# Key, key, sum, sum: regrouping the steps of a cross-attention loop on four engines, and a rewritten opening

## The reference

```
lat = layer_norm(latents, ln_lat_g, ln_lat_b)
ctx = layer_norm(context, ln_ctx_g, ln_ctx_b)
q = (lat @ Wq)                    # 16 heads of 64
k, v = split(ctx @ Wkv)           # 1024 tokens per batch
k = apply_rope(k, cos, sin)       # rotation of the two halves of each head
attn = clip(q k^T * scale, -11, 11); attn = softmax(attn)
out = (attn v) @ Wo + bo
```

## Time and profile before

| | |
|---|---|
| median of 3 runs | 1251.46 us (1250.63 to 1252.29) |
| the profiled execution | 1255.13 us, of it 1253.4 us span |
| PE busy | 95% of the span |
| DVE / POOL / ACT busy | 78% / 56% / 52% |
| opening, up to the first scores | 67.4 us |
| loop of the steps | to about 960 us |
| linear attention, then experts | to about 1073 us, then to the end |

### The profile page before, as it was taken

One profiled execution on the slowest core, in us unless ns is written; L12 is line 12 of the kernel. 1 busy time (PEld: TensorE's weight loads), 2 busy tenths in 40 slices (PEclk: granted clock), 3 DMA queues, 4 the chain that ended last, 5 costly groups with the idle time before them and its releaser, 6 DMA issues.

```text
span 1253.4 us, 39825 instructions
## 1 busy us (share of the span) xinstructions
PE 1191.6 (95%) x16268; PEld 1003.6 (80%) x16268; DVE 981.2 (78%) x1954; ACT 646.7 (52%) x1089; POOL 700.2 (56%) x611
## 2 busy tenths in 40 slices
PE   7798999999999999999999999999999999899997
PEld 3576878878877888778878878778878888789997
DVE  6489878878878888888888878778868366668886
ACT  7364455655545545555555545555435233356664
POOL 2374767757667766667767756666434123333333
PEclk8899999999999999999999999999999999999999
DMA  6264656656555665556655656655654441566662
GB/s 228 51 160 109 164 134 149 156 138 153 137 132 140 159 155 138 144 139 160 152 132 141 162 136 149 148 133 132 156 126 110 148 157 36 186 182 194 203 189 68
DMA packets 136173, 181.36 MB, mean 145 GB/s; under 512 B 30316, under 2 KB 96312, under 8 KB 135864
## 3 DMA queue, kind: packets, MB, share of 16 engines
q1 hardware_dynamic: 110552, 150.80, 45.5%
q10 hardware_dynamic: 21360, 23.80, 7.5%
q0 software_dynamic: 4080, 4.22, 1.6%
HBM read 81.93 MB, written 30.56 MB: 90 GB/s over the span
## 4 chain that ended last, share of the span: by engine, by line
PE 87%; issue 3%; DVE 3%; ACT 2%; DMA 2%; POOL 1%; SPq 1%; POOLq 0%; ACTq 0%; DVEq 0%
PE bank L1560 29%; PE bank L1589 27%; PE bank L1546 10%; PE bank L1915 6%; PE bank L1612 3%; PE bank L1719 2%; PE bank L1965 2%; PE bank L1966 1%; PE bank L1967 1%; PE bank L1772 1%; PE bank L1647 1%; PE bank L1815 1%; PE bank L1796 1%; DMA w_two<-in_L_ffn_W_dram 1%; DMA x_slots<-xn_all,slot 1%
## 5 line engine op out<-in xcount | busy, mean ns | idle before, releaser
L1560 PE MATMUL bank<-ct,wk_hi 128*128 128x512 f32 x1024 | 332.7, 407 | 11.0 <-DVE ct L1117 4.2
L1589 PE MATMUL bank<-p_hi,xc 128*128 128x512 f32 x1024 | 316.0, 390 | 0.0
L597 POOL TENSOR_TENSOR kr<-kr,ksw 128x1024 f32<-128x1024 f32 x64 | 154.7, 2417 | 186.8 <-issue 140.3
L1107 DVE TENSOR_TENSOR kw<-bank,stab 128x512 f32<-128x512 f32 x256 | 176.4, 689 | 100.7 <-PE bank L1560 95.3
L1560 PEld LDWEIGHTS bank<-ct,wk_hi 128*128 128x128 f32 x1024 | 192.9, 193 | 53.5 <-issue 8.8
L1589 PEld LDWEIGHTS bank<-p_hi,xc 128*128 128x128 f32 x1024 | 191.8, 188 | 39.8
L1560 PE MATMUL bank<-ct,wk_lo 128*128 128x512 f32 x512 | 204.9, 400 | 0.0
L1589 PE MATMUL bank<-p_lo,xc 128*128 128x512 f32 x512 | 199.2, 389 | 0.0
L779 ACT CAST p_hi<-pr 128x1024 fp32r<-128x1024 f32 x128 | 133.7, 1045 | 88.1 <-DVE pr L1075 87.8
L609 POOL TENSOR_TENSOR xc<-raw,xc 128x255 fp32r<-128x255 f32 x128 | 167.0, 1304 | 1.3 <-ACT xc L742 1.3
L1095 DVE TENSOR_TENSOR p_lo<-pr,p_hi 128x1024 fp32r<-128x1024 f32 x128 | 165.6, 1294 | 0.5 <-ACT p_hi L779 0.5
(11 more groups left out here) (227 smaller groups left out, 1994.9 us busy)
## 6 DMA issues: line engine op xcount, KB each, us to landing
ksw<-kw SPq DMA_DIRECT2D x512, 128.0 KB, 2.3
x_turned<-xt SPq DMA_DIRECT2D x120, 128.0 KB, 3.3
ct_read<-x_turned SPq DMA_DIRECT2D x30, 512.0 KB, 5.1
w_two<-in_L_ffn_W_dram SPq DMA_DIRECT2D x15, 1024.0 KB, 5.1
raw<-in_ctx_dram ACTq DMA_DIRECT2D x56, 256.0 KB, 3.6
x_slots<-fill ACTq DMA_DIRECT2D x32, 258.0 KB, 3.8
w_all<-in_L_ffn_W_dram SPq DMA_DIRECT2D x4, 2048.0 KB, 16.9
wo<-in_L_ffn_W_dram SPq DMA_DIRECT2D x7, 1024.0 KB, 5.0
```

The costliest lines, as they stand in the source:

```text
L597: pool.tensor_tensor(kr_at(j + 2), kr_at(j + 2), ksw[:, i], ALU.add).then_inc(kr_done, 1)
L1107: dve.tensor_tensor(by_tile(kw[:, i, cols]), keys_, by_tile(stab[:, places]), ALU.mult).then_inc(kw_done, 1)
L1560: last = pe.matmul(psK[:, a * 512:(a + 1) * 512], l[:, k, w], ct[:, h % 3, r, k], start=(m == 0), stop=(m == len(parts) - 1))
L1589: last = pe.matmul(psZ[c], xc[:, slot_, l, t, cols], r[:, i, :, t], start=(f == 0 and m == 0), stop=(f == 1 and m == len(parts) - 1), skip ...
```

## The change

It moves instructions and changes one wait; no instruction is added or taken away.

- PE, `two_steps`: keys(j+4), keys(j+5), sums(j-2), sums(j-1).
- DVE, `two_steps`: the four `keys_turned` stand in one run; `clamped(j+1)` and `weights_low(j)` come behind them; the odd step's `blocks_turned` moves behind the pair's end, to the head of the next pair; `half_low` comes ahead of `weights_low(j+1)`.
- POOL: the two sums of a pair (`keys_summed`) stand together ahead of the small work (`deviations`) and the low rows (`rows_low`). The first of them waits for `clamp_done` of the pair's first step instead of for `k_ps`, the second for neither.
- the opening: on PE keys(0) stands ahead of the context tile 6, query slices lie between keys(1) and keys(2); ACT, DVE and POOL are written out to match.

```
@@ POOL
-            def step(j):
+            def keys_summed(j):
                 if there(j + 2):
                     pool.wait_ge(ku_done, 2 * (j + 3))
-                    if j >= 0:
-                        if there(j + 4):
-                            pool.wait_ge(k_ps, 2 * (j + 4) + 1)
-                        else:
-                            pool.wait_ge(clamp_done, j + 1)
+                    if j >= 0 and j % 2 == 0:
+                        pool.wait_ge(clamp_done, j + 1)
                     pool.wait_ge(sw_ld[i], ((j + 2) // 2 + 1) * 64)
...
+            for j in range(-5, 0):
+                deviations(j)
+                rows_low(j)
+                keys_summed(j)
+            for j in range(0, STEPS, 2):
+                keys_summed(j)
+                keys_summed(j + 1)
+                for a in range(2):
+                    deviations(j + a)
+                    rows_low(j + a)
@@ ACT, opening
-            opening(-3)
+            rows_high(-4)
+            context_high(6)
+            queries(7, 0)
+            context_high(7)
+            normalised(-4)
+            queries(0, 1)
+            rows_high(-3)
             act.wait_ge(w_last_ld, 32)
             act.activation(w_last[:], w_last[:], ACT.Identity, scale=g_last[:]).then_inc(bias_done, 1)
-            opening(-2)
-            queries(7, 0)
-            queries(0, 1)
-            opening(-1)
             queries(1, 1)
+            normalised(-3)
+            rows_high(-2)
             queries(2, 1)
+            normalised(-2)
+            rows_high(-1)
             queries(3, 1)
+            normalised(-1)
+            loads(-1)
@@ DVE
             def two_steps(j):
+                blocks_turned(j - 1)
                 if due(j, 8):
                     added((j - 8) // 4)
...
                 keys_turned(j, 0)
                 keys_turned(j, 1)
+                keys_turned(j + 1, 0)
+                keys_turned(j + 1, 1)
                 clamped(j + 1)
                 weights_low(j)
                 blocks_turned(j)
...
                 counted(j + 1)
-                keys_turned(j + 1, 0)
-                keys_turned(j + 1, 1)
-                weights_low(j + 1)
-                blocks_turned(j + 1)
                 if half_written(j - 1):
                     half_low(half_written(j - 1))
+                weights_low(j + 1)
@@ DVE, opening
+            keys_turned(-4, 0)
+            keys_turned(-4, 1)
+            context_low(5)
+            shifts(-3)
+            counted(-3)
+            keys_turned(-3, 0)
+            keys_turned(-3, 1)
+            context_low(6)
+            blocks_turned(-3)
+            context_low(7)
+            query_weights_low(1)
...
@@ PE
                 keys(j + 4)
+                keys(j + 5)
                 sums(j - 2)
-                keys(j + 5)
                 sums(j - 1)
...
-            turn_context(6)
             pe.wait_ge(q_act, 6)
             pe.wait_ge(wk_lo_done, 2)
             keys(0)
+            turn_context(6)
             keys(1)
+            queries(7, 0)
             turn_context(7)
-            queries(7, 0)
             queries(0, 1)
+            queries(1, 1)
             keys(2)
-            queries(1, 1)
             queries(2, 1)
             keys(3)
             queries(3, 1)
...
             keys(4)
+            keys(5)
             queries(4, 1)
             queries(5, 1)
-            keys(5)
```

53 lines of the change are left out of this document (23 added, 30 removed).

## The result

The changed kernel takes **1296.95 us** (median; 1293.06 to 1300.1), the kernel before beside it 1251.05. The ratio is 1.037, with an interval of 1.033 to 1.041: 46 us slower, where the forecast was 16 and its range ended at 1290. The sign was right, the size was not. The profiled execution is 1297.26 us, of it 1295.5 span; before it was 1255.13 and 1253.4.

What follows compares the result with a forecast made beforehand. PE's own stream bounds the loop; the opening has real gaps. Terms -9.5 - 4 + 16.5 + 13 = +16 on the median 1251.5 gave 1267.5 us, range 1244 to 1290 (forecast's own 1259 to 1278).

Steps and rivals of the forecast that it cites:

- `o_part`: Loop, keys behind outputs: late x_turned delays `added`, so keys wait 1.0 us in 13 of 29 pairs; +13 us (0 to 28).
- DVE did not become the bound: Loop: a rival had DVE becoming the bound or the clock falling, +24, 1291 us; chance 0.18.
- the first scores end near 60: Opening: both first scores end at 60.0 us instead of 69.5, after waiting for POOL's sum.
- Rival 1: Loop: x_turned lands 4 us from first issue, so `added` is in time; 1254.5 us, chance 0.20.
- Keys on keys: Loop, second keys directly behind first: PE waits for DVE's reading, 0.3 us in about 55 pairs; +16.5 us (8 to 25).
- The worry that the clock would fall more often: Loop, in the rival at 1291 us (chance 0.18): waits before keys plus shorter issue gaps drop PE's clock, 1.8 us each.
- Issue gaps: Loop, inside the scores: gaps stay unchanged because scores and outputs keep their places in PE's stream; 0 us.
- The first pairs: First pairs after the opening: 4 of 6.8 us of PE's waits for DVE and low clock gained; -4 us (0 to -7).
- The opening: Up to the first scores' end: the new order fills PE's gaps; -9.5 us (-12 if POOL's sum is not late, -5 with low clock).

Runs made afterwards that it cites:

- e12: Kernel before with one added wait: SP issues the four x_turned DMAs only when the pair's second keys have run on PE; 1249.85 us (1.0021).
- e5: Changed kernel with DVE's even transpose at the pair's head, x_turned DMAs ahead of the even ksw, ct_read between the two ksw; 1263.22 us (1.0106).
- e10: e5 with two matmuls of sums(j-2) set between keys(j+4) and keys(j+5) on PE; 1244.5 us (0.9974).
- e4: Kernel before with the new opening alone on all engines, and the old loop; 1238.34 us (0.9921).
- e1: Changed kernel with DVE's even-step transpose moved from behind the rotations to the head of the pair; 1274.18 us (1.0227).
- e8: Kernel before with GpSimd's part of the change alone: two sums in one run, the first behind the clamp; 1299.12 us (1.0391).

## Why the prediction was wrong

**Right.** PE's loop was the bound and lost what it gained ahead of it; the wait behind outputs ends with DVE's `o_part` at S+2.8 or later, by the chain of transposes, x_turned and `added`; DVE did not become the bound; the first scores end near 60 (61.3), with POOL's sum as the last wait. Rival 1, the DMA in time, is out for this kernel: it landed 5.3 us from its first issue (median of 28), against 5.0 in the forecast and 5.1 before. What the Trainium skill says in "Perfetto Trace Analysis", section "DMA Instruction — HWDGE (DVE, Sync)", that the completion of writes to HBM can come surprisingly late, agrees with that. But e12 shows that it isn't a constant. In the old loop, issued 3.6 us ahead of the scores (changed kernel 2.8, before 5.3; medians), the same writes were there in 4.4 us, and `o_part` in time. SP and DVE of e12:

```profile
606.84 2.30 SPq L436 DMA_DIRECT2D x_turned<-xt  x4
```

```profile
611.21 0.45 DVE L1072 STREAM_TRANSPOSE xt<-raw 128x256 f32<-128x256 f32 x1 [1.70 <-DMA x_turned<-xt]
```

**Wrong, term by term** (forecast, measured):

- *`o_part`: +13, +23.0.* Two factors. The step that took the wait as 1.0 us in each pair was short: it is 1.45 where it is paid, since the landing is 0.3 us later than 5.0 and the issue 0.2 later than I had it (medians). And the 13 of 29 pairs rested on 16 gap pairs hiding the wait. One of the 16 was miscounted, since its gap (1.76 us at 526.89) lies inside the keys and hides nothing ahead of them; of the other 15 only 11 are left, so 18 pairs have no cover, and 16 of them pay. Three pairs more at 1.0 us are 3 of the 10 us that were missing; the longer wait is the other 7.
- *Keys on keys: +16.5, about +20.5* (e5 to e10). The mechanism was right: 0.18 of waiting and a fresh start. But it is 0.35 a pair and not 0.3, and it was paid in about all 58 pairs and not in 55. The remaining 14.0 us behind the keys (34.5 - 20.5) are nearly those of before (15.0): in both kernels 5 pairs are below the full clock, and e4, where none is, still has 6.8. The worry that the clock would fall more often did not come true.
- *Issue gaps: 0, +5.1.* The step "the gaps stay, since scores and outputs stand at the same places of PE's stream" failed in both halves. The places stayed, but four gaps vanished and the others grew by half. What is fixed in the stream is where a new block of PE's instructions begins; the gap's length, and whether there is one, go with the end of the 16 KB packet on the `instruction` queue, and its start moved from 0.90 us ahead of the gap to 0.13 behind it (seven gaps). The profile of before already had the queue and its packets, and the forecast read "issue" as waiting for nothing that the profile names. The DMA load beside the scores grew as well (share 1.09 and 0.91 in the second and third microsecond behind their start, mean of the 29 pairs; before 0.53 and 0.37); that this delayed the packets is not shown. In e1 the x_turned writes go out 6.1 us ahead of the scores, but `ct_read` (512 KB) then goes out beside their start, and the gaps stay at 31.0.
- *The first pairs: -4, +1.6.* PE's waits in the opening and the first pairs, from its timeline (compare):

```profile
37.72 0.73 PE L1578 MATMUL bank<-ct,wk_hi 128*128 128x512 f32 x2 [0.35 <-DVE kr_third L1118]
45.65 0.70 PE L1578 MATMUL bank<-ct,wk_hi 128*128 128x512 f32 x2 [0.25 <-DVE ct L1123]
59.77 1.54 PE L1564 MATMUL bank<-qo,kr 64*64 64x64 f32 x64 [4.62 <-POOL kr L594]
81.28 0.74 PE L1578 MATMUL bank<-ct,wk_hi 128*128 128x512 f32 x2 [2.05 <-DVE kr L1118]
97.23 0.73 PE L1578 MATMUL bank<-ct,wk_hi 128*128 128x512 f32 x2 [2.48 <-DVE kr_third L1118]
```

  The long waits for `ct` of the earlier trace rows are gone, but in the first pairs two for the readings (2.05 and 2.48) took their place: with both keys in a row, a late DVE meets PE within one half instead of within three. I had priced what goes and not what this lateness meets next. The waits for DVE are still less than before in sum (4.5 us, before 0.51, 1.24 and 3.69). What makes it +1.6 is keys on keys (some 0.35 in each of the four pairs up to scores(8)) and the low clock, met twice (granted clock 0.90 in 61.3:73.8 and in 89.7:107.2) where it was met once (0.91 in 108.9:128.3).
- *The opening: -9.5, -8.2.* As forecast, 1.3 us short, by the one wait of 4.62 for POOL.
- Not in the sum: +1.0 behind the loop, and 4 us because the profiled execution of before lay above its median and that of after does not.

The terms add to +16, the measured ones to 42 (-8.2 + 1.6 + 23.0 + 5.1 + 20.5 - 1.0 + 1.0). Of the 26 between them 10 are in `o_part`, 5.1 in the gaps and 5.6 in the first pairs. The terms were not independent: the late DVE feeds both `o_part` and the first pairs, and the fate of the instruction packets sets both the gaps and how many pairs they cover. The range let each bound stand by itself, and was too narrow at the top.

## What to carry to other kernels

Put the consumer's and the producer's runs side by side: a second product into a bank that is read between needs other work of at least the reader's lag in between, and two matmuls (0.45 us) were enough here to save 20 us. When the profile says "issue", look at the `instruction` queue before calling the gap fixed: here each such gap ended 0.9 to 1.6 us behind a 16 KB packet of it, so its length is the packet's lateness. A gap that hides a wait is cover only as long as it stays, so a term that counts on it needs the case without it as its upper end.

## What the runs showed of the hardware

PE's issue gaps in runs of small matmuls are waits for its instructions: 239 gaps in 17 traces, each ending 0.9 to 1.6 us behind a 16 KB packet of the `instruction` queue, each 193 or 194 instructions into a block of 256. They are fixed in place and not in length: the same seven were 1.5 to 1.9 us in seven kernels with the old loop and few DMAs on them, and 2.5 to 3.2 in three with the new loop and DMAs at a share of 0.8 to 1.1. GpSimd's sum of two 128x1024 operands held up DVE's one-input clamp from 0.68 to 2.44 us (e8; the clamp at 392.13), and not the products that read PSUM (0.68 and 0.69 in e8 as in the kernel before). The landing of the four 128 KB x_turned writes, from the first issue, was 5.1 us before, 4.4 in e12 and 5.3 in the changed kernel (medians), with 4.1 and 7.3 as ends.
